# Quantised layer of a four-layer decoder: first half's input normed and quantised amid the attention, blocks in one interleaved order, last rounding pass on ScalarE

## What is computed

```python
# attention (32 heads of 8, 8 key groups): causal and padded softmax, then w_o, b_o
x = x + _L2_xattn_ref(_layernorm(x), ctx_2048, ctx_2048, mask_BxS2_if1, L2_xattn_w_q, ...)
x = x + _L2_ffn_ref(_layernorm(x), L2_ffn_w_gate, L2_ffn_w_up, L2_ffn_w_down)

def _rmsnorm(x):
    return x * jax.lax.rsqrt(jnp.mean(x * x, axis=-1, keepdims=True) + RMS_EPS)
def _act_quant(x):        # per token: 127 over the row's largest magnitude
    scale = 127.0 / jnp.clip(jnp.max(jnp.abs(x), axis=-1, keepdims=True), EPS)
    q = jnp.round(jnp.clip(x * scale, -128.0, 127.0)) / scale
    ...
def _weight_quant(w):     # per matrix: to -1, 0, 1 by the mean magnitude
    scale = 1.0 / jnp.clip(jnp.mean(jnp.abs(w)), EPS)
    q = jnp.round(jnp.clip(w * scale, -1.0, 1.0)) / scale
    ...
def _bitlinear(x, w):
    xq = _act_quant(_rmsnorm(x)); wq = _weight_quant(w)
    return jnp.einsum('bsi,oi->bso', xq, wq)
gate = jax.nn.silu(_bitlinear(x, w_gate))
up = _bitlinear(x, w_up)
return _bitlinear(gate * up, w_down)      # hidden width 1024
```

## Time and profile before

| | us |
|---|---|
| median of 3 runs | 1685.01 |
| lowest, highest | 1681.39, 1688.26 |
| the profiled execution | 1674.45 |
| its span, first to last instruction | 1672.7 |
| last attention product ends, by the trace | 1257.0 |
| last statistics of the quantised layer end | 1318.7 |

### The profile page before, as it was taken

The page is one execution under the profiler, slowest core; times in us unless marked ns, Lnnn a source line. Parts: engine busy times, 40 slices in busy tenths (PEclk is TensorE's granted clock), DMA queues, the critical chain, the costliest instruction groups (busy, mean ns, idle before and its releaser), DMA issues.

```text
span 1672.7 us, 25668 instructions
## 1 busy us (share of the span) xinstructions
PE 1480.9 (89%) x9775; PEld 918.5 (55%) x9792; DVE 1000.1 (60%) x1792; ACT 730.4 (44%) x1740; POOL 416.8 (25%) x353
## 2 busy tenths in 40 slices
PE   4879999998999879999989979689994788999788
PEld 2535555555566446565557855465552545555536
DVE  5694222225577767767775767736768676575531
ACT  2262111112666556565653545347765453253220
POOL 1040000000000187777770000000191135224100
PEclk8988999999999989999999989899998899999989
DMA  7020121003000300000001000010001100000000
GB/s 234 1 101 1 62 57 29 0 0 151 1 2 2 115 7 7 7 7 7 7 1 70 1 21 0 1 76 2 2 2 65 52 0 3 2 1 2 27 0 26
DMA packets 21645, 48.11 MB, mean 29 GB/s; under 512 B 1426, under 2 KB 16787, under 8 KB 20372
## 3 DMA queue, kind: packets, MB, share of 16 engines
q1 hardware_dynamic: 21524, 46.47, 8.0%
HBM read 41.22 MB, written 5.24 MB: 28 GB/s over the span
## 4 chain that ended last, share of the span: by engine, by line
PE 65%; DVE 22%; ACT 5%; issue 4%; POOL 3%; DMA 0%; SPq 0%; DVEq 0%; ACTq 0%; POOLq 0%
PE PS L683 49%; PE PS L875 5%; DVE work L2110 4%; PE PS L745 4%; PE PS L913 2%; DVE work L2059 2%; PE PS L1158 2%; DVE small L1697 2%; PE PS L695 1%; DVE WA L2026 1%; POOL XN L662 1%; PE PS L957 1%; DVE small L2037 1%; DVE small L2039 1%; PE PS L1184 1%
## 5 line engine op out<-in xcount | busy, mean ns | idle before, releaser
L683 PE MATMUL PS<-XT,WB 128*128 128x512 f32 x656 | 300.2, 608 | 0.0
L683 PEld LDWEIGHTS PS<-XT,WB 128*128 128x128 f32 x656 | 126.3, 195 | 142.8 <-issue 141.2
L1412 ACT ACTIVATE work<-PS,small 128x128 f32<-128x128 f32 x512 | 140.7, 416 | 72.7 <-DVE small L1932 72.3
L532 POOL TENSOR_SCALAR small<-small 128x4 f32<-128x4 f32 x22 | 5.6, 252 | 531.6 <-DVE small L1700 531.6
L1906 DVE TENSOR_TENSOR work<-PS,work 128x512 f32<-128x512 f32 x48 | 33.1, 692 | 171.2 <-PE PS L683 171.2
L683 PE MATMUL PS<-XT,WA 128*128 128x512 f32 (+1 forms) x248 | 113.9, 612 | 2.2 <-DVEq L2113 2.1
L1368 ACT ACTIVATE work<-PS 128x512 f32<-128x512 f32 x48 | 28.7, 597 | 194.8 <-PE PS L683 194.8
L1932 DVE TENSOR_REDUCE small<-PS 128x4 f32<-128x512 f32 x128 | 82.3, 685 | 37.2 <-PE PS L683 37.2
L662 POOL TENSOR_TENSOR XN<-work,WB 128x512 f32<-128x512 f32 x64 | 67.4, 1071 | 123.7 <-PE PS L683 123.7
L683 PE MATMUL PS<-WA,XT 128*128 128x256 f32 (+2 forms) x416 | 87.1, 370 | 4.7 <-DVE XT L1952 3.0
L2110 DVE SCALAR_TENSOR_TENSOR work<-PS,vec,work 128x508 f32<-128x508 f32 (+2 forms) x108 | 80.2, 743 | 13.1 <-DVE work L2110 6.4
(11 more groups left out here) (359 smaller groups left out, 2945.1 us busy)
## 6 DMA issues: line engine op xcount, KB each, us to landing
WB<-in_l0f SPq DMA_DIRECT2D x8, 768.0 KB, 7.8
WB<-in_l1x SPq DMA_DIRECT2D x1, 6144.0 KB, 17.5
WB<-in_l0f SPq DMA_DIRECT2D x32, 96.0 KB, 6.9
WB<-in_l2f SPq DMA_DIRECT2D x1, 3072.0 KB, 11.3
WA<-in_l3a SPq DMA_DIRECT2D x1, 2624.0 KB, 9.2
WB<-in_l3f SPq DMA_DIRECT2D x1, 2064.0 KB, 7.7
WA<-in_l1f SPq DMA_DIRECT2D x1, 2056.0 KB, 10.0
C<-in_ctx SPq DMA_DIRECT2D x2, 1024.0 KB, 7.8
```

Source lines behind the costliest of these rows:

```text
L683: mm = lambda o, l, r, s, e: nc.tensor.matmul(o, l, r, start=s, stop=e)
L1412: f(wk(12288 + (u % 8) * G + h * P, P), bank(j)[:, h * P:(h + 1) * P], ACT.Exp, bias=sm(704 + (u % 8) * 4 + h, 1)).then_inc(*act_step(*([j ...
```

## The change

- The first group's input is normed and quantised during the attention. VectorE runs `quantise_input(0, step)` with the steps 0 to 4 at the head of rounds 23 to 27 (`QUANT_AT`). As the attention's queries are in `XN`, the group's values go to `C`, the context's tile, which nothing reads then. GpSimd makes the group's roots (`input_roots(0)`) ahead of its nine weight passes. TensorE's two transposes of the group stand between the last `pv` and the last `o` of the attention.
- The second group is quantised by VectorE after the products of block 0.
- The blocks run in one order (`quantised_order`): gate and up of blocks 6 and 7 come behind the transposes of the hidden values of block 0, and behind the down product of block 0. VectorE scales the hidden values of block b-5 after the products of block b, the last four between the residual additions.
- The second pass over the hidden values (large number off, to bf16) is done by ScalarE (`whole`, an Identity with a bias), no longer by VectorE.

```diff
 SUMS_AT = 20
+QUANT_AT = 23
...
-    l = [("qt", g, c) for g in range(2) for c in range(2)] + \
-        [(k, b, h) for b in range(NB) for h in range(2) for k in ("gate", "up")]
-    for b in range(NB + 1):
-        if b < NB:
-            l += [("ht", b)]
-        if b >= 1:
-            l += [("o", b - 1)]
+    l = []
+    for what, b in quantised_order():
+        if what == "in":
+            l += [(k, b, h) for h in range(2) for k in ("gate", "up")]
+        else:
+            l += [("qt", 1, 0), ("qt", 1, 1)] if what == "qt" else [(what, b)]
...
+        if sums_at is not None and r == PAIRS + 1:
+            l += [("qt", 0, 0), ("qt", 0, 1)]
+    return l
...
+def quantised_order():
+
+
+    l = [("in", 0), ("in", 1), ("in", 2), ("in", 3), ("qt", 1), ("in", 4), ("in", 5)]
+    for b in range(NB + 1):
+        if b < NB:
+            l += [("ht", b)]
+        if b >= 1:
+            l += [("o", b - 1)]
+        if b < 2:
+            l += [("in", 6 + b)]
     return l
...
+        def l2f_normed(g):
+
+            return C[:, 0:1024] if g == 0 else XN[:, 1024:2048]
+
+        def l2f_whole(g):
+
+            return C[:, 1024:1536].bitcast(BF16) if g == 0 else wkb(8704, 1024)
+
+        def l2f_xt(g):
+
+            return C[:, 1536:2048].bitcast(BF16) if g == 0 else wkb(9216, 1024)
...
+            input_roots(0)
             pool.wait_ge(weight_scales, 1)
             done = 0
...
+            input_roots(1)
...
+                pe.wait_ge(dve_to_pe.sem, dve_to_pe.next())
+                for c in range(2):
+                    o = begin(layer, "qt", g, c).bitcast(BF16)
+                    for i in range(4):
+                        ins = nc.tensor.transpose(o[:, i * P:(i + 1) * P], l2f_whole(g)[:, i * D + c * P:i * D + (c + 1) * P], identb[:, :])
...
+            for what, b in quantised_order():
+                if what == "qt":
...
+                if what == "in":
+                    g, t = b // 4, b % 4 * P
...
+                if what == "ht":
+                    pe.wait_ge(whole_hidden.sem, whole_hidden.next())
...
-                if b >= 1:
-                    o = begin("l2f", "o", b - 1)
-                    pe.wait_ge(*freed(J("l2f", "ht", b - 1)))
+                if what == "o":
+                    o = begin("l2f", "o", b)
+                    pe.wait_ge(*freed(J("l2f", "ht", b)))
...
+            def whole(b):
+                act.wait_ge(scaled_hidden.sem, scaled_hidden.next())
+                f(wkb(14336, 8192)[:, b * 1024:(b + 1) * 1024], wk(b * 1024, 1024), ACT.Identity, bias=less_magic).then_inc(*act_step(whole_hidden))
+
...
+            for b in range(NB + 6):
+                if b == 4:
+                    quantised_evac("l2f", 1)
+                if b < NB:
+                    gates(b)
+                if 1 <= b <= NB:
+                    squares(b - 1)
+                if 5 <= b < NB + 5:
+                    whole(b - 5)
+                if b >= 6:
+                    hidden_evac(b - 6)
...
+            def quantise_input(g, step):
+
+                normed = l2f_normed(g)
+                if step == 0:
+                    roots(g)
+                    dve.wait_ge(*dve_last())
+                    for i in range(4):
+                        b = 4 * g + i
+                        v.tensor_scalar(normed[:, i * D:(i + 1) * D], X[:, b * D:(b + 1) * D],
+                                        sm(64 + 2 * b, 1), sm(88 + b, 1), ALU.subtract, ALU.mult).then_inc(*dve_step())
+                if step == 1:
+                    v.tensor_reduce(sm(160 + 4 * g, 4), r3(normed, D), AX.X, ALU.max, apply_absolute_value=True).then_inc(*dve_step())
+                if step == 2:
+                    activation_scales(g)
+                    dequant(g, 184, 0)
+                    dequant(g, 192, 1, input_scales)
+                if step == 3:
+                    for i in range(4):
+                        xb = normed[:, i * D:(i + 1) * D]
+                        v.tensor_scalar(xb, xb, sm(168 + 4 * g + i, 1), MAGIC, ALU.mult, ALU.add).then_inc(*dve_step())
+                if step == 4:
+                    v.tensor_scalar(l2f_whole(g), normed, MAGIC, None, ALU.subtract).then_inc(*dve_step(dve_to_pe))
+                dve.wait_ge(*dve_last())
...
+            def scale_hidden(b):
+
+                hb = wk(b * 1024, 1024)
+                v.tensor_scalar(hb, hb, sm(168 + b, 1), MAGIC, ALU.mult, ALU.add).then_inc(*dve_step(scaled_hidden))
+                dve.wait_ge(*dve_last())
...
                     if key[0] == "s":
                         u = key[1]
+                        if layer == "l2x" and u % 2 == 0 and 0 <= u // 2 - QUANT_AT < 5:
+                            quantise_input(0, u // 2 - QUANT_AT)
                         j = J(layer, "s", u)
...
+            for b in range(NB + 1):
+                if b < NB:
+                    products(b)
+                if b == 0:
+                    for step in range(5):
+                        quantise_input(1, step)
+                if b >= 5:
+                    scale_hidden(b - 5)
             for b in range(NB):
...
+                if b == 2:
...
+                if b >= 2 and b + 2 < NB:
+                    scale_hidden(b + 2)
+                scaled_residual("l2f", b, 200)
```

More of the change, by code:

```diff
@@ L1582, in _, with gates @@
             heads("l2x")
[L1585 to L1596 removed]
+            def gates(b):
                 for h in range(2):
@@ new lines, in products @@
+            def products(b):
+                for h in range(2):
+                    dve.wait_ge(act_to_dve.sem, act_to_dve.next())
+                    j = J("l2f", "up", b, h)
+                    dve.wait_ge(*full(j))
+                    v.scalar_tensor_tensor(wk(b * 1024 + h * G, G), bank(j), sm(192 + b, 1), wk(10240 + h * G, G),
+                                           ALU.mult, ALU.mult).then_inc(*dve_step(j))
+                dve.wait_ge(*dve_last())
+                dve.sem_inc(dve_to_act.sem, dve_to_act.give())
+                v.tensor_reduce(sm(160 + b, 1), wk(b * 1024, 1024), AX.X, ALU.max, apply_absolute_value=True).then_inc(*dve_step())
+                if b == 4:
+                    activation_scales(0)
+                    dequant(0, 200, 2)
+                dve.wait_ge(*dve_last())
@@ L2253, in _ @@
-            for b in range(NB):
-                if b == 4:
+            for b in range(NB + 1):
[6 more added lines that the diff above has]
+                    scale_hidden(b - 5)
+            for b in range(NB):
+                if b == 2:
                     activation_scales(1)
```

187 lines of the change are left out of this document (77 added, 110 removed).

## The result

The changed kernel takes 1723.49 us (median of 4 runs, 1718.39 to 1730.24), the kernel before 1683.20 (4 runs, 1677.05 to 1688.26): a ratio of 1.0236, 95% interval 1.0209 to 1.0262, so it is slower by 40 us. The forecast was 1717, within 1690 to 1729. The profiled execution of the changed kernel took 1722.92 us (span 1721.1), near its median; that of the kernel before, 1674.45, was 9 us under its own.

A forecast was written before the change was run, and what follows sets the result against it. TensorE was taken to pace the attention, with VectorE's input quantising behind it. Median 1685.0 us plus 32.3 (attention waits for GpSimd passes 30.3, quantised layer 2.0) gave 1717 us, range 1690 to 1729.

The forecast's parts named there:

- one VectorE instruction for each end of a GpSimd pass: Attention: VectorE's SBUF-to-SBUF or two-SBUF-input instructions wait for GpSimd's pass to end, and one gets in before the next.
- Step 0: Round 23: means-roots product and four normalising instructions wait for five pass ends; maxima begin at 1238.7 instead of 1215.3.
- step 3: Round 26's inserted VectorE instructions: find GpSimd idle and take 1.14 us, on the path of that round.
- Step 2: Round 25's inserted VectorE instructions: wait for the last passes, to 1253.2, plus 0.4; maxima 31.1 us late.
- It stays near 30 as long as step 2 meets the last pass: Attention: condition for its 30.3 us delay, given round 25's inserted instructions wait for the end of GpSimd's weight work.
- the 14.7 us from the front: Input quantising behind the attention, which the change hides; claimed to come back later in the layer, net 0.
- ring: Layer blocks 6 and 7: hand-overs among ScalarE, TensorE and VectorE, taking 6.9 and 8.3 us instead of 2.7.
- tail: Layer's end: last four blocks scaled, passed, copied, multiplied and added at 2.6 to 3.1 us each, ending at 61.6.
- five places of slow clock: Layer's ring and tail: TensorE slower at five places, some 0.4 us each, adding 2.0 us.
- Slow passes let VectorE in: Attention rival: 7.08 and 5.38 us passes don't hold VectorE, only 2.00 us passes might; 1689 us, chance (none) 0.13.
- Only some hold: Attention rival: 5.38 us passes hold VectorE, 7.08 us ones don't; some 9 us instead of 30, 1696 us, chance 0.12.
- Nothing blocks: Rival: no hold in the attention and most of 14.7 us stays saved in the layer; 1675 us, chance (faster) 0.07.

The follow-up runs named there:

- experiment 10: Kernel before, plus 21 small VectorE scalings (128x256), one ahead of each of scores 42 to 62, beside whole GpSimd weight passes: 1718.53 us.
- experiments 7: Changed kernel with each of GpSimd's nine weight passes cut into four pieces of 512 columns: 1700.79 us, ratio 1.0070.
- 8: Changed kernel with each of GpSimd's nine weight passes cut into two pieces of 1024 columns: 1699.93 us (one run).
- 11: Kernel before, plus 21 small VectorE scalings, with each GpSimd weight pass cut into two pieces of 1024 columns: 1691.82 us.
- experiment 6: Changed kernel with weight passes ahead of the inserted steps, and the second rounding pass back on VectorE, pipeline kept: 1693.66 us, ratio 1.0041.
- experiments 2: Changed kernel with straight block order in the layer and both rounding passes on VectorE, attention unchanged: 1715.78 us, ratio 1.0167.
- 4: Changed kernel with early weight passes, straight order, and second rounding on ScalarE only for blocks 5 to 7: 1683.67 us, ratio 0.9985.
- 12: Changed kernel with early weight passes, straight order, rounding split 5 to 3, and input steps in portions where VectorE waits: 1678.61 us, ratio 0.9943.
- experiment 1: Changed kernel with GpSimd's nine weight passes brought ahead of VectorE's inserted steps, same layer: 1698.67 us, ratio 1.0071.
- experiment 3: Changed kernel with early weight passes, straight layer order and both rounding passes on VectorE: 1685.22 us, ratio 0.9986.
- experiments 9: Kernel before, plus eight VectorE instructions of several kinds on an idle buffer during GpSimd's nine weight passes: 1696.87 us (one run).

## Why the prediction was right, step by step

**What bounds, and the place of the cost: right.** The reading of the earlier trace rows, that a scaling waits for the end of GpSimd's instruction, holds for nine of nine in experiment 10. TensorE sets the attention's pace, and VectorE's delay turns into TensorE's holes, as named.

**Attention, +30.3 forecast, +28.9 measured: the sum was right, its distribution was not.** The step "one VectorE instruction for each end of a GpSimd pass" failed twice. The product of means and roots is an instruction with two SBUF inputs, which is let in after 4.35 us of 7.08; and the third scaling slipped into the 0.1 us between two passes. Step 0 so took three pass ends (1225.6, 1231.1 and 1233.3), not five: the maxima of round 23 were late by 11.0 us (20.6 behind those of round 20 in place of 9.7), not by 23.4. In return step 3, which I had put behind the last pass, met the last two and took 12.16 us in place of 1.14. Step 2, six instructions and not the seven that I had counted, took 6.2 us for my 8.4. The holes were 8.3 us at step 0 and 12.1 at step 3, not one of 15 to 20 at step 0 and one of 5 at step 2. The total came out all the same, since it hangs on one number: VectorE is through when the ninth pass is. I had that 47.0 us behind the scales' product (1206.2 to 1253.2); it was 47.2 (1213.4 to 1260.6). "It stays near 30 as long as step 2 meets the last pass" was a lucky form of the right thought: some step had to.

The Trainium skill, "SBUF — State Buffer", section "Who interferes with whom", calls the port pair that the two engines share an exclusive lock, which a VectorE instruction in a two-port mode, as scalings can be, and a GpSimd instruction keep from each other for the whole instruction, and says that a VectorE instruction with two SBUF inputs contends with a GpSimd instruction that reads SBUF. For a scaling beside a pass of 2048 columns the trace agrees (nine ends of nine within 0.15 us); for two SBUF inputs (let in 4.35 us into 7.08) and for pieces of 1024 or 512 columns (experiments 7, 8 and 11) it is not held for the whole instruction, and the measurement decides.

**Layer, +2.0 forecast, +5.7 measured: the mechanism was right, two sizes off.** That the 14.7 us from the front come back in ring and tail, so that nothing is won, held: the same kernel with a straight order, and the second pass on VectorE, gives the layer in 55 us. But the loss lies outside my own bounds of 0 to +5: the turns took 8.55 and 10.4 us (transposes at 1322.96, 1331.51 and 1341.90) where I had 6.9 and 8.4. I had counted five places of slow clock at 0.4 us. In one turn alone the transposes take 1.03 instead of 0.61, the down products 1.87 instead of 1.04, and the eight gate and up products 3.1 us, of which I had 0.5 on the path. The granted clock over the layer was 0.75 where it had been 0.83 before. The tail was 19.8 us for my 19.3. The second size was the rounding on ScalarE, 1.15 us where I took the squares' 1.06, and worth 4.2 us of layer as experiment 6 shows.

**The rivals.** "Slow passes let VectorE in" is out for scalings, and true in part for instructions with two SBUF inputs, which are let in 4.35 us into a pass of 7.08. That alone saves little here, since the scalings behind them are held. "Only some hold" is out: in experiment 10 passes of all three kinds held to their end. "Nothing blocks" is out. What that rival had of the layer comes true in part by another order: in experiments 2 to 4 and 12, 6.6 to 8.7 of the 14.7 us stay gone.

**What was not forecast at all.** From the two stages I get +34.6 us, the times say +40.3. Nearly every experiment shows the same: +8.1 by the stages and +11.4 measured in experiment 1, -5.0 and -2.0 in experiment 3; only in experiment 12 do the two agree. One cause can be named: the profiled execution of the kernel before was one of its fastest. Three later profiles (experiments 9, 10 and 11) have its code ahead of round 20 and from the quantised layer on. There round 20 begins at 1211.4 to 1213.2 us, in the kernel before at 1205.7, in the changed one at 1212.8. The stretch behind the layer takes 360.7 to 360.9, 354.0 and 360.8; the layer itself 61.9 us in all three, for 61.6. So these profiles show no slower code behind the changed layer, and the layer before is at most 0.3 us longer than I took it. The times scatter too: the four runs of the kernel before beside the changed one gave 1683.2, the later comparisons, with 15 to 23 runs each, 1686.6 to 1687.5, against which the changed kernel is 36 to 37 us slower. Experiment 1 came out 8 us above its 1691 for the same two reasons, 4 us by the base that I had counted from (1683 for 1687.3) and 3 by which its time exceeds its stages. Those some 3 us, which most experiments have, stay open.

## What to carry to other kernels

Before work of VectorE is moved beside GpSimd, look at the length of GpSimd's single instructions and at the kind of VectorE's: even an SBUF-to-SBUF scaling of four numbers a partition costs what is left of the pass (4.7 us in experiment 9), and the engines that wait for VectorE pay. Cutting the passes (90% of the hold gone with pieces of 512 columns, at 14% more GpSimd time) or moving them takes it away. Before blocks are interleaved over several engines, add up the chain through one turn: here each turn was a closed chain of 10.3 us where the busiest engine had 6.0 us of work, and the order lost. Where an engine's next input hangs on the output of its last, try the straight order, and look for the win in what is taken off the front.

## What the runs showed that I had not expected

- A scaling is held to the end of a 2048-column pass of any of the three kinds, but only for about the first 0.9 and the last 0.6 to 0.8 us of a 1024-column piece of 2.77 or 3.63 us, with the same engines, buffers and operations. Why the middle opens when the instruction is half as long is open; no run here separates column count from bytes or duration.
- An instruction with two SBUF inputs and one output is held for 4.35 us of a pass of 7.08 (three cases, within 0.02 us) for both sizes tried, 128x512 and 128x4. In a pass of 5.37 the one case was held for about 3.5 (line 1999 above).
- Nine passes in 36 pieces took 50.5 us in place of 44.2, in 18 pieces 46.3.
